# Two edits in an eight-core attention and FFN kernel: the first two token blocks computed four chunks wide, by quarters of the contraction, and five w2 tiles loaded ahead of the second half of FFN2's input

## The reference, cut to what matters

```python
q, k, v = x @ Wq.T + bq, x @ Wk.T + bk, x @ Wv.T + bv      # 2048, 512, 512 wide
sq, sk = elu(q) + 1, elu(k) + 1
kv = einsum('bhsd,bhse->bhde', sk, v); k_sum = sk.sum(axis=2)
attn = einsum(sq, kv) / (einsum(sq, k_sum) + 1e-6)
x = layernorm(x + attn @ Wo.T)
w1_q, w2_q = ternary(w1), ternary(w2)     # sign where |w| >= 0.7 * mean|w|, else 0
h = gelu(x @ w1_q.T + b1)                 # 8192 wide
x = layernorm(x + h @ w2_q.T + b2)
```

## Time and profile before

| | |
|---|---|
| runs shown | 2474.5, 2669.95 and 2840.87 us (median 2669.95) |
| profiled execution | 2475.41 us |
| its span (core 6, the slowest) | 2473.9 us |
| spans of the eight cores | 2462.2 to 2473.9 us |
| mean granted clock of the cores | 0.991 to 0.995 |
| PE busy | 2393.8 us, 97% |
| DVE, ACT, POOL busy | 50%, 29%, 22% |

### The profile page before, as it was taken

How to read it: one execution, slowest core, us unless ns; L and a number is a source line. 1 busy time by engine, 2 the same in 40 slices (tenths; PEclk the granted TensorE clock), 3 DMA queues, 4 the chain that set the end, 5 groups by cost and what they waited for, 6 DMA issues and landing times.

```text
span 2473.9 us, 31808 instructions; the slowest of 8 cores (2462.2 to 2473.9 us)
## 1 busy us (share of the span) xinstructions
PE 2393.8 (97%) x11158; PEld 1094.0 (44%) x11300; DVE 1243.9 (50%) x1395; ACT 725.6 (29%) x1109; POOL 552.1 (22%) x419
## 2 busy tenths in 40 slices
PE   4999999999999999999999999889999999999997
PEld 1444444444444444444444444334444444444443
DVE  1222344445567777777788886466647301200021
ACT  0233577753313566666533333000000000000000
POOL 3000000004335444343434343011112101100000
PEclk9999999999999999999999999989999999999999
DMA  9994587696555787778544445977668577722253
GB/s 158 216 240 159 156 204 197 169 265 250 225 206 198 245 272 258 268 261 264 197 148 163 148 161 206 311 266 265 204 206 259 174 252 249 235 72 68 86 198 117
DMA packets 106955, 507.01 MB, mean 205 GB/s; under 512 B 12976, under 2 KB 12976, under 8 KB 69808
## 3 DMA queue, kind: packets, MB, share of 16 engines
q1 hardware_dynamic: 50400, 323.55, 39.3%
q0 software_dynamic: 27600, 124.80, 19.4%
q10 hardware_dynamic: 28800, 56.64, 7.3%
HBM read 444.11 MB, written 98.57 MB: 219 GB/s over the span
## 4 chain that ended last, share of the span: by engine, by line
PE 91%; DMA 6%; DVE 2%; issue 1%; POOL 0%; ACT 0%; SPq 0%; DVEq 0%; POOLq 0%; ACTq 0%
PE PB L862 29%; PE PB L773 29%; PE PB L700 8%; PE PB L737 8%; PE PB L876 4%; PE PB L674 4%; PE PB L664 4%; PE PB L764 2%; DMA MA<-w2h 2%; DMA R<-woh 2%; DMA RW<-wvh 2%; DMA hd<-R 1%; PE PB L716 1%; PE PB L689 0%; PE PB L687 0%
## 5 line engine op out<-in xcount | busy, mean ns | idle before, releaser
L862 PE MATMUL PB<-R 128*128 128x512 fp8e4 x2576 | 567.8, 384 | 17.2 <-DVE R L969 17.2
L773 PE MATMUL PB<-R,RW 128*128 128x512 bf16 x2351 | 534.2, 379 | 2.6
L862 PEld LDWEIGHTS PB<-R 128*128 128x128 bf16 x2576 | 254.1, 99 | 329.6 <-issue 32.2
L773 PEld LDWEIGHTS PB<-R,RW 128*128 128x128 fp8e4 x2400 | 234.8, 98 | 282.9
L580 POOL TENSOR_TENSOR RW<-MC 128x1024 fp8e4<-128x1024 fp8e4 x120 | 246.1, 2083 | 283.3 <-DVE MC L969 283.3
L1104 DVE TENSOR_TENSOR MC<-PB,MC 128x512 f32<-128x512 f32 x56 | 38.3, 684 | 416.4 <-PE PB L862 231.7
L700 PE MATMUL PB<-R,MB 128*128 128x512 bf16 x1003 | 229.5, 379 | 1.1
L773 PE MATMUL PB<-R,MC 128*128 128x512 bf16 x942 | 225.2, 379 | 0.9
L862 PE MATMUL PB<-R,RW 128*128 128x512 fp8e4 x784 | 170.4, 379 | 0.0
L966 DVE TENSOR_SCALAR MB<-MA,thr 128x2048 fp8e4<-128x2048 f32 x102 | 138.0, 1353 | 51.4 <-DMA MA<-w2h 40.8
L969 DVE SCALAR_TENSOR_TENSOR MC<-MA,thr,MB 128x2048 fp8e4<-128x2048 f32 x64 | 158.3, 2473 | 7.0 <-DVE MB L966 0.5
(11 more groups left out here) (134 smaller groups left out, 2517.3 us busy)
## 6 DMA issues: line engine op xcount, KB each, us to landing
MA<-w1h SPq DMA_DIRECT2D x126, 1024.0 KB, 6.3
MB<-w2h SPq DMA_DIRECT2D x108, 512.0 KB, 7.3
MA<-w2h SPq DMA_DIRECT2D x45, 1024.0 KB, 7.9
MC<-w2h SPq DMA_DIRECT2D x19, 1024.0 KB, 7.2
...
```

The source lines that it names most:

```text
L773: ins = e.matmul(PB[m_bank(u, i)], w[:, dc * 128:(dc + 1) * 128], x[:, dc * 512:(dc + 1) * 512], start=(dc == 0), stop=(dc == 7))
L862: ins = e.matmul(PB[F2_BANK[P][cc]], hid(fc, P)[:, cc * 128:(cc + 1) * 128], w2q_sb(s, g, q)[:, j * 512:(j + 1) * 512], start=(fc == 0), s ...
```

## The change

**In the first stage** the first 8 chunks are computed by another loop nest. A function quarter(blk, q, w, done) runs, for all four chunks of a block, the 4 matmuls of one quarter of the contraction, into banks 0 to 3. Block 0 goes K quarters 0 to 3, then V quarters 0 to 3, then block 1 the same, with the short products of chunk q behind K quarter q of block 1. K and V of a block use the same four banks, so V's first quarter waits chunk by chunk for DVE's addition (v_kb), and K's first quarter of block 1 for V's eviction (v_sv). Ahead of all stands a wait for the second quarter of Wk and x. Block 1 has a semaphore for each quarter (d_xq). From sc = 8 on the loop is the old one; chunk 8 also carries the products of chunks 4 to 7. kb1, sk_sb and sv_sb of the first 8 chunks lie in MA and at the start of MB, four of each. Since MA is the staging memory of the weight tiles, SP's first load_w now waits for v_sk >= 8 and t_kv >= 8, and since the start of MB is that of the Wq tiles, POOL waits for t_kv >= 8 before it issues these. W_KV0 is 8, and w_behind_kv spreads the 26 tiles over 24 chunks: one each, and two at sc = 19 and sc = 31.

**In FFN2** SP loads w2 tiles 10 to 14 before the last 0.5 MB of half 0 and the four pieces of half 1. Behind these, tile 15 + i now follows piece i; before, tile 10 + i preceded it.

```diff
--- before.py
+++ after.py
@@ -22,7 +22,7 @@
 NSC = 32
 NCH = 16
 NFC = 64
-W_KV0 = 6
+W_KV0 = 8
 NW_KV = 26
 NW_Q = 32
 NW_WO = 16
@@ -38,8 +38,8 @@
 
 def w_behind_kv(sc):
 
-    a = sc - W_KV0
-    return range(a, a + 1) if 0 <= a < NW_KV else range(0)
+    a, n = sc - W_KV0, NSC - W_KV0
+    return range(NW_KV * a // n, NW_KV * (a + 1) // n) if a >= 0 else range(0)
 
 
 def w_behind_q(n):
@@ -168,15 +168,24 @@
     b8t = mb8[:, 8 * KB:10 * KB]
 
     def kb1(sc):
+        if sc < 8:
+            return maf[:, (sc % 4) * 512:(sc % 4 + 1) * 512]
+        return kb(sc)
+
+    def kb(sc):
         return mbf[:, 3072 + (sc % 2) * 512: 3072 + (sc % 2 + 1) * 512]
 
     def ek(sc):
         return mcf[:, (sc % 2) * 512:(sc % 2 + 1) * 512]
 
     def sk_sb(sc):
+        if sc < 8:
+            return mab[:, 4096 + (sc % 4) * 512: 4096 + (sc % 4 + 1) * 512]
         return mcb[:, 2048 + (sc % 2) * 512: 2048 + (sc % 2 + 1) * 512]
 
     def sv_sb(sc):
+        if sc < 8:
+            return mbb[:, (sc % 4) * 516:(sc % 4 + 1) * 516]
         o = 4096 + (sc % 2) * 516
         return mcb[:, o:o + 516]
 
@@ -189,7 +198,7 @@
     wres = mcf[:, 2752 + NW_ALL:2752 + NW_ALL + NW_COL2]
 
     def eq(n):
-        return kb1(n)
+        return kb(n)
 
     def rn(m):
         return ek(m)
@@ -298,7 +307,7 @@
         return [sem(f"{name}{i}") for i in range(n)]
 
     d_bq, d_b1, d_bk, d_bv, d_b2 = [sem(n) for n in ("d_bq", "d_b1", "d_bk", "d_bv", "d_b2")]
-    d_wk, d_wv, d_x0 = sems("d_wk", 4), sems("d_wv", 4), sems("d_x0_", 4)
+    d_wk, d_wv, d_x0, d_xq = sems("d_wk", 4), sems("d_wv", 4), sems("d_x0_", 4), sems("d_xq", 4)
     d_x = sems("d_x", 8)
     d_st = sems("d_st", 3)
     d_h = sems("d_h", 3)
@@ -406,7 +415,8 @@
         e.dma_start(out=bvbc, in_=bv).then_inc(d_bv, 16)
         e.dma_start(out=bq_sb, in_=bq).then_inc(d_bq, 16)
         e.dma_start(out=b1_sb, in_=b1).then_inc(d_b1, 16)
-        e.wait_ge(t_k, W_KV0 - 1)
+        e.wait_ge(v_sk, 8)
+        e.wait_ge(t_kv, 8)
         def load_hid(P, half, a, b, signal):
             e.wait_ge(d_hs[2 * P + half], n_hs((b - 1) // 2))
             e.dma_start(out=hid_rows(a, b, half),
@@ -480,6 +490,9 @@
         e.wait_ge(t_m, n_m(63, M3))
         load_w2(W2_PRE + 2)
         load_hid(0, 0, 36, 60, d_ha[2])
+
+        for r in range(W2_PRE + 3, 15):
+            load_w2(r)
         e.wait_ge(d_hs[2], n_hs(31))
         e.wait_ge(d_hs[3], n_hs(31))
         load_hid(0, 0, 60, 64, d_ha[3])
@@ -487,9 +500,9 @@
         e.wait_ge(a_h, n_h(63, H22))
         e.wait_ge(d_hs[1], n_hs(31))
         for i in range(4):
-            load_w2(W2_PRE + 3 + i)
             load_hid(0, 1, 16 * i, 16 * i + 16, d_hb[i])
-        for r in range(W2_PRE + 7, 64):
+            load_w2(15 + i)
+        for r in range(19, 64):
             load_w2(r)
 
         e.wait_ge(t_z, 28)
@@ -532,7 +545,9 @@
                         base=0, channel_multiplier=1).then_inc(p_id)
         for blk in range(1, 8):
             for q in range(4):
-                e.dma_start(out=x_quarter(blk, q), in_=xb[blk, q]).then_inc(d_x[blk], 16)
+                e.dma_start(out=x_quarter(blk, q), in_=xb[blk, q]).then_inc(
+                    d_xq[q] if blk == 1 else d_x[blk], 16)
+        e.wait_ge(t_kv, 8)
         for ic in range(2):
             e.dma_start(out=wq_sb(ic), in_=wqh[ic]).then_inc(d_wq[ic], 16)
         e.wait_ge(v_sv, NSC)
@@ -650,27 +665,52 @@
                                start=(sc == 0), stop=(sc == NSC - 1))
             ins.then_inc(t_kv)
 
-        for sc in range(NSC):
+
+        def quarter(blk, q, w, done):
+            for c in range(4):
+                if q == 0 and w is wv_sb:
+                    e.wait_ge(v_kb, 4 * blk + c + 1)
+                elif q == 0 and blk == 1:
+                    e.wait_ge(v_sv, c + 1)
+                for dc in range(4 * q, 4 * q + 4):
+                    ins = e.matmul(PB[c], x_oth(blk, dc)[:, c * 128:(c + 1) * 128], w(dc),
+                                   start=(dc == 0), stop=(dc == 15))
+                if q == 3:
+                    ins.then_inc(done)
+
+        e.wait_ge(d_wk[1], 16)
+        e.wait_ge(d_x0[1], 16)
+        for q in range(4):
+            e.wait_ge(d_wk[q], 16)
+            e.wait_ge(d_x0[q], 16)
+            quarter(0, q, wk_sb, t_k)
+        for q in range(4):
+            e.wait_ge(d_wv[q], 16)
+            quarter(0, q, wv_sb, t_v)
+        for q in range(4):
+            e.wait_ge(d_xq[q], 16)
+            quarter(1, q, wk_sb, t_k)
+            kv_products(q)
+        for q in range(4):
+            quarter(1, q, wv_sb, t_v)
+
+        for sc in range(8, NSC):
             blk, cc = sc // 4, sc % 4
             xs = x_oth if blk < 4 else x_own
-            if sc >= 2:
+            if sc < 10:
+                e.wait_ge(v_sv, sc - 3)
+            else:
                 e.wait_ge(v_kb, sc - 1)
-            if blk >= 1 and cc == 0:
+            if cc == 0:
                 e.wait_ge(d_x[blk], 64)
             for dc in range(16):
-                if sc == 0 and dc % 4 == 0:
-                    e.wait_ge(d_wk[dc // 4], 16)
-                    e.wait_ge(d_x0[dc // 4], 16)
                 ins = e.matmul(PB[sc % 2], xs(blk % 4, dc)[:, cc * 128:(cc + 1) * 128], wk_sb(dc),
                                start=(dc == 0), stop=(dc == 15))
             ins.then_inc(t_k)
-            if sc >= 1:
-                kv_products(sc - 1)
-            if sc >= 2:
-                e.wait_ge(v_sv, sc - 1)
+            for k in range(4, 8) if sc == 8 else (sc - 1,):
+                kv_products(k)
+            e.wait_ge(v_sv, sc - 1)
             for dc in range(16):
-                if sc == 0 and dc % 4 == 0:
-                    e.wait_ge(d_wv[dc // 4], 16)
                 ins = e.matmul(PB[2 + sc % 2], xs(blk % 4, dc)[:, cc * 128:(cc + 1) * 128], wv_sb(dc),
                                start=(dc == 0), stop=(dc == 15))
             ins.then_inc(t_v)
@@ -885,28 +925,53 @@
         e.memset(c_eps_at, EPS_ATTN).then_inc(v_init)
         e.memset(c_eps_ln, EPS_LN).then_inc(v_init)
         e.memset(ones, 1.0).then_inc(v_init)
-        for sc in range(2):
+        for sc in (0, 1, 2, 3, 8, 9):
             e.memset(sv_sb(sc), 1.0).then_inc(v_init)
         e.wait_ge(d_bk, 16)
         e.tensor_scalar(bk1bc, bk1bc, 1.0, None, ALU.add).then_inc(v_init)
         e.wait_ge(d_bq, 16)
         e.tensor_scalar(bq1_sb, bq_sb, 1.0, None, ALU.add).then_inc(v_init)
-        e.wait_ge(v_init, 8)
+        e.wait_ge(v_init, 12)
         e.wait_ge(d_bv, 16)
         bv3 = bvbc.rearrange("p (h e) -> p h e", h=4)
-        for sc in range(NSC):
+
+        def add_bk(sc, bank):
             e.wait_ge(t_k, sc + 1)
-            if sc >= 2:
+            if 4 <= sc < 8:
+                e.wait_ge(v_sk, sc - 3)
+            elif sc >= 10:
                 e.wait_ge(v_sk, sc - 1)
-            e.tensor_tensor(kb1(sc), PB[sc % 2], bk1bc, ALU.add).then_inc(v_kb)
+            e.tensor_tensor(kb1(sc), PB[bank], bk1bc, ALU.add).then_inc(v_kb)
+
+        def make_sk(sc):
             e.wait_ge(v_kb, sc + 1)
             e.wait_ge(a_e, sc + 1)
-            if sc >= 2:
+            if 4 <= sc < 8:
+                e.wait_ge(t_kv, sc - 3)
+            elif sc >= 10:
                 e.wait_ge(t_kv, sc - 1)
             e.scalar_tensor_tensor(sk_sb(sc), ek(sc), 1.0, kb1(sc), ALU.min, ALU.max).then_inc(v_sk)
+
+        def make_sv(sc, bank):
             e.wait_ge(t_v, sc + 1)
+            if 4 <= sc < 8:
+                e.wait_ge(t_kv, sc - 3)
+            elif sc >= 10:
+                e.wait_ge(t_kv, sc - 1)
             e.tensor_tensor(sv_sb(sc).rearrange("p (h e) -> p h e", h=4)[:, :, 0:128],
-                            PB[2 + sc % 2].rearrange("p (h e) -> p h e", h=4), bv3, ALU.add).then_inc(v_sv)
+                            PB[bank].rearrange("p (h e) -> p h e", h=4), bv3, ALU.add).then_inc(v_sv)
+
+        for b in range(2):
+            for sc in range(4 * b, 4 * b + 4):
+                add_bk(sc, sc % 4)
+            for sc in range(4 * b, 4 * b + 4):
+                make_sk(sc)
+            for sc in range(4 * b, 4 * b + 4):
+                make_sv(sc, sc % 4)
+        for sc in range(8, NSC):
+            add_bk(sc, sc % 2)
+            make_sk(sc)
+            make_sv(sc, 2 + sc % 2)
         e.wait_ge(t_kv, NSC)
         for h in range(4):
             e.tensor_copy(kvsb[:, h * 128:(h + 1) * 128], PB[4 + h][:, 0:128]).then_inc(v_kvev)
```

## The result

| | before | after |
|---|---|---|
| runs compared, us | 2474.5, 2482.1 | 2446.47, 2447.2, 2449.43 |
| profiled execution, its span | 2475.41, 2473.9 (core 6) | 2446.47, 2444.9 (core 3) |
| spans of the cores | 2462.2 to 2473.9 | 2432.4 to 2444.9 |

The median of the three runs after is 2447.2 us. The ratio is 0.9877, with a 95% interval of 0.9838 to 0.9915: 1.2% faster, less than the 2% that counts as a difference here. From profile to profile the gain is 28.9 us, where I had forecast 40.7.

A forecast was written before the change was run, and what follows sets the result against it. PE was taken as the bound, busy 97% of the span, leaving only its waits and slow-clock stretches to win. First stage 13.5 us (19.1 - 5.6) plus FFN2 27.2 makes 40.7 off 2475.4: 2435 us, range 2427 to 2450.

The forecast's parts named there:

- After that it heals: K and V stage after chunk 9: later weight loads have 12.2 us against 11.3 measured, so no further PE loss.
- the 3.2 us for each MB: FFN2's start: pace of SP's queue, from 3 MB in some 9.6 us, used to time the w2 tile landings.
- The start: K and V stage: PE starts at 21.41 us, V of block 0 ends at 51.2, block 1 at 79.8; 19.1 us gained.
- The stall at chunk 9: Product of chunk 9: first weight tile lands at 97.1, PE waits 3.6 us and restarts slowly; 5.6 us lost.
- ACT's waits for weight tiles go on past chunk 12: K and V stage: a sign, named beforehand, that the prediction is wrong.
- the 4 us of room: Chunk 19, two tiles summed: ACT ends about 2 us past its chunk, the exponential has some 4 us of room.
- FFN2, tiles 10 to 14: FFN2's first pass: these w2 tiles, loaded ahead, are made by 1575 to 1590.5 us, each 7 us early for PE.
- FFN2, tile 15: End of FFN2's first pass: tile made by 1600 to 1602, wanted at 1601.0; 0.5 us lost, for a 27.2 us gain.
- POOL's stores share the engines: FFN2: reason given for the rival in which the wait only moves, chance 0.10.
- FFN2's wait only moves: Rival, chance 0.10: tile 15 or a half-1 piece takes over the wait; half of 27.7 us back gives 2449 us.
- Half 1's first piece: FFN2: behind five w2 tiles it lands at 1593 us, wanted by PE at 1604.4, so it holds.
- The ACT chain: Rival, chance 0.03: weight-tile landings and sums pace the whole K and V stage; 2501 us, slower than before.

The follow-up runs named there:

- part1: The first-stage edit alone, with FFN2's loads in the order of the kernel before; 2459.06 us, ratio 0.9951 against before.
- part2: The kernel before with only the FFN2 edit of SP's loads; 2454.15 us, ratio 0.9930 against before.
- late_double: The changed kernel with the second doubled weight tile summed at chunk 27 in place of 19; 2440.52 us, ratio 0.9874 against before.
- lead: The changed kernel with weight tiles summed from chunk 10 on, doubles at chunks 25, 27, 29 and 31; 2436.32 and 2437.52 us, ratio 0.9855 against before.
- stores_late: The changed kernel with POOL's stores of w2 tiles 9 to 15 held back until tile 15 is made; one run, 2445.94 us.

## Why the prediction was right or wrong

2447.2 us lies inside my range, near its slow end; the gain of 28.9 us is 71% of the 40.7 forecast. Both edits gain where I said they would, and part1 and part2 show that they add. Each gave less than I said, 12.6 us for 13.5 and 17.5 for 27.2 in kernels of their own. Two steps failed: "After that it heals" in the first stage, and the 3.2 us for each MB in FFN2's sum, which is the larger.

- **The start.** First matmul 21.84 (forecast 21.4), V of block 1 ends at 80.80 (79.8), chunk 8 as forecast. 1.0 us off.
- **The stall at chunk 9** was where I put it, with ACT waiting for its first tile at 97.15 (forecast 97.1) and the second landing by 103.37 (103.0). Its size was over-forecast: 1.9 us and no clock lost, for 3.6 + 2.0. The worst core of after has 2.66 and 1.7 of clock, and the same core of late_double 2.94 and 1.1 (4.75 for 3.62). On core 3 the time that this over-forecast saved offset most of the next error; that is luck.
- **"After that it heals"** is the step of the first stage that failed. I gave later loads 12.2 us of room against 11.3, and they did take 11.5, so it healed, but far too slowly: the exponential of chunk 10 began 6.0 us behind the end of its K, that of chunk 19 still 2.1, and each sum up to there began only when its tile landed, 3 to 5 us into ACT's idle time. That "ACT's waits for weight tiles go on past chunk 12" was one of my own signs of being wrong, and they went on to 190.7 us. In that state the second tile of chunk 19 costs not its sum, 2 us, but the wait for its own landing as well: 7.28 us. Of these the 4 us of room that I named took a part, and the rest, 3.35 us with 1.7 of lower clock, reached PE. late_double removed exactly this stall, and lead both.
- **FFN2, tiles 10 to 14.** Forecast made 41.4 us after FFN2's start (1590.5), 7 us ahead of PE; they were made by 1583.7, 45.6 us after it. PE wanted the last at 1586.4. The margin shrank to 2.7 us and still held, so they cost nothing.
- **FFN2, tile 15** is the term that was mis-sized. I took 3.2 us for each MB from one stretch of 9.6 us, a 2 MB piece and a tile. My own spoke against it: PE's waits of 1590.90 and 1622.56, three such groups apart, make 10.6 us a group or 3.5 us for each MB. Over the whole stretch before it was 288 GB/s (3.6 us), and with POOL's and ACT's queues moving 2.05 MB in 36 us, where they had moved 1.58 in 58, it became 254 (4.1 us). Tile 15 could go out only when tile 12 was made, 4 us later than in the sum, and landed 17.3 us after that; PE waited 7.4 and lost 1.7 to the clock: 9.1 us for my 0.5. I had written "POOL's stores share the engines" under a rival with a chance of 0.10, and taken nothing of it into the sum. stores_late shows that share: 268 to 292 GB/s on one core, and 1.6 to 6.8 us less of PE's wait on four. What makes up the rest of the pace stays open. The 9.1 us are the rival "FFN2's wait only moves", come true to a third of the 27.7 us where it said half.
- The 2449 of that rival is close to the measured time by luck: it had one of two reasons, and that at the wrong size. 8.7 of the missing 11.8 us are FFN2's, 2.9 the first stage's.
- Half 1's first piece landed 52.0 us after FFN2's start, where I had 44, and PE wanted it at 55.3. It held here; with tile 15 ahead of it too it no longer does.
- The ACT chain did not set the pace of the stage: PE ran from chunk to chunk at 7.15 us but for two places.

The rule of the Trainium skill that I weighed, page "DMA: Bandwidth & Descriptors", section "Two DMAs through the same engine are not ordered", is that transfers in one queue start in order but are pipelined; by my reading it might have brought the tiles earlier. They came later than my sum, and on core 3 of after the pieces and tiles from 1538.9 to 1576.1 us landed in the order of their issue.
